# One token tower on one core: the counting products of the expert router are issued behind the probability transposes, and their results are read behind the first normalisation

## The reference

```python
h = _L0_tok_ref(x, W, b, class_token, pos_embed)           # patches @ W.T + b, class token, + pos_embed
h = h + _L0_attn_ref(_layernorm(h), w_qkv, w_proj, b_proj)  # 12 heads of 16, keys within 6 tokens
h = h + _L0_ffn_ref(_layernorm(h), router_w, w1, b1, w2, b2)

# _L0_ffn_ref
probs = softmax(flat @ router_w.T)
top_w, top_i = top_k(probs, 2);  top_w = top_w / top_w.sum(-1)
for e in range(8):
    w_e = sum(top_w * (top_i == e))
    out = out + w_e * (gelu(flat @ w1[e] + b1[e]) @ w2[e] + b2[e])
```

## Time and profile before

| | |
|---|---|
| median of 3 runs | 1693.18 us (1689.94 to 1693.35) |
| the profiled execution | 1697.55 us, of which its span is 1695.8 us |
| TensorE busy | 1491.4 us, 88% of the span |
| weight loads | 1238.1 us, 73% |
| VectorE busy | 1121.2 us, 66% |
| GpSimd busy | 861.2 us, 51% |
| ScalarE busy | 718.4 us, 42% |

### The profile page before, as it was taken

How to read it: one execution, slowest core, us unless ns; L and a number is a source line. 1 busy time by engine, 2 the same in 40 slices (tenths; PEclk the granted TensorE clock), 3 DMA queues, 4 the chain that set the end, 5 groups by cost and what they waited for, 6 DMA issues and landing times. The chain is left out here.

```text
span 1695.8 us, 52298 instructions
## 1 busy us (share of the span) xinstructions
PE 1491.4 (88%) x18345; PEld 1238.1 (73%) x18346; DVE 1121.2 (66%) x2875; ACT 718.4 (42%) x1201; POOL 861.2 (51%) x900
## 2 busy tenths in 40 slices
PE   4777999999999999899562799999999999999995
PEld 4666888888888788788451577777777777777774
DVE  3466777778777776777645466666666666666663
ACT  2443444444444444444421444444444444444441
POOL 3122656656555555555535155545554555455544
PEclk9887999999999999999865799999999999999998
DMA  6654555555555555555422334443444334433432
GB/s 206 205 172 126 157 148 154 153 151 155 144 150 154 150 152 145 143 139 150 113 76 95 93 59 60 60 65 57 59 60 65 57 59 60 65 58 59 59 45 29
DMA packets 190164, 182.64 MB, mean 108 GB/s; under 512 B 86361, under 2 KB 166437, under 8 KB 188989
## 3 DMA queue, kind: packets, MB, share of 16 engines
q1 hardware_dynamic: 125834, 111.46, 23.7%
q0 software_dynamic: 41680, 41.84, 16.8%
q10 hardware_dynamic: 22499, 27.28, 4.9%
HBM read 104.93 MB, written 65.29 MB: 100 GB/s over the span
## 5 line engine op out<-in xcount | busy, mean ns | idle before, releaser
L988 POOL DMA_INDIRECT out<-y,token x219 | 368.5, 1683 | 73.7 <-issue 72.9
L1096 PE MATMUL down<-w_hi,g_hi 128*128 x1314 | 323.7, 246 | 1.9 <-DVE y L1062 1.1
L1098 PE MATMUL down<-w_hi,g_lo 128*128 x1314 | 323.0, 246 | 0.0
L1097 PE MATMUL down<-w_lo,g_hi 128*128 x1314 | 322.9, 246 | 0.0
L1084 PE MATMUL up<-e_xT,w_hi 128*128 128x384 f16 x1314 | 286.7, 327 | 0.0
L1009 ACT ACTIVATE act_out<-up,bias 128x384 f32<-128x384 f32 x438 | 250.9, 581 | 73.3 <-PE up L1084 73.2
L391 POOL DMA_INDIRECT sorted_scratch<-payload,place x212 | 219.5, 1035 | 59.9 <-issue 56.9
L775 PE MATMUL near<-we,patches 128*120 128x192 f32 x1272 | 226.2, 335 | 17.4 <-DMA patches<-in_xt 10.0
L1001 ACT COPY e_xT<-turned 128x1152 f16<-128x1152 f16 x73 | 81.6, 1118 | 353.8 <-PE turned L1076 353.8
L775 PEld LDWEIGHTS near<-we,patches 128*120 128x120 f32 x1272 | 210.2, 187 | 27.8 <-issue 27.7
L1045 DVE TENSOR_TENSOR g_lo<-act_out,g_hi 128x768 f16<-128x768 f32 x219 | 209.9, 958 | 7.6
(11 more groups left out here) (154 smaller groups left out, 2745.9 us busy)
## 6 DMA issues: line engine op xcount, KB each, us to landing
patches<-in_xt SPq DMA_DIRECT2D x53, 720.0 KB
rows<-sorted_scratch SPq DMA_DIRECT2D x73, 301.5 KB, 2.8
v_diag<-v_scratch SPq DMA_DIRECT2D x159, 89.2 KB
v_scratch<-v_rows SPq DMA_DIRECT2D x53, 191.2 KB, 3.0
tab<-tab_scratch SPq DMA_DIRECT2D x53, 180.0 KB
out<-h ACTq DMA_DIRECT2D x52, 180.0 KB
stage<-in_w ACTq DMA_DIRECT2D x8, 1152.0 KB
k_diag<-qk SPq DMA_DIRECT2D x424, 15.8 KB
```

The lines of the kernel that those rows point to most:

```text
L988: pool.indirect_dma_start(out=out, out_offset=bass.IndirectOffsetOnAxis(ap=token[k][:, n:n + 1], axis=0), in_=y[k % 2][:, n, :], in_offset ...
L1096: pe.matmul(dst, g_hi[k % 2][:, m, cols], high, start=(m == 0), stop=False)
L1097: pe.matmul(dst, g_hi[k % 2][:, m, cols], low, start=False, stop=False)
L1098: ins = pe.matmul(dst, g_lo[k % 2][:, m, cols], high, start=False, stop=(m == MF - 1))
```

## The change

On TensorE the block under `if counted:` moves from behind the embedding to behind the turning of the probabilities: behind three groups of transposes. On VectorE the two operations of route part 2 move from ahead of the first normalisation to behind it. Nothing is added or dropped; the semaphores and their values are the same. At t = 8 to 52 all three groups of transposes exist. At t = 54 and 56 there is no turning of xs, at t = 58 and 60 none of the three, and VectorE's first normalisation exists only up to t = 52, so that part 2 moves only there.

```diff
@@ vector, body(t)
                     statistics(h1[f % H_RING], st1, mv1, "1", f + 1)
-                if due:
-                    route_steps(grp, 2)
                 if runs(t, 0):
                     normalise(h1[f % H_RING], mv1, rs1, xn1, "1", f + 1)
...
                 if due:
+                    route_steps(grp, 2)
                     route_steps(grp, 3)
@@ tensor, body(t): the three blocks of transposes now stand ahead of the counting
+                if runs(t, 1):
+                    ...
+                    turn(xs1, token_bank[:].bitcast(F16), ...).then_inc(s["turned1"], 1)
+                if runs(t, 5):
+                    ...
+                    turn(os_, far[:].bitcast(F16), ...).then_inc(s["o_turned"], 1)
+                if runs(t, 4):
+                    pe.wait_ge(s["exp_set"], c + 1)
+                    ...
+                        ins.then_inc(s["prob_turned"], 1)
                 if counted:
                     pe.wait_ge(s["marks_set"], grp + 1)
...
                     ins.then_inc(s["counted"], 1)
-                if runs(t, 1):
-                    ...
-                if runs(t, 5):
-                    ...
-                if runs(t, 4):
-                    ...
                 if runs(t, 6):
```

More of the change, by code:

```diff
@@ L785, in body @@
                 grp, counted = groups(t, 8)
[L786 to L796, removed]
                 if runs(t, 1):
@@ L814, in body @@
                         ins.then_inc(s["prob_turned"], 1)
+                if counted:
+                    pe.wait_ge(s["marks_set"], grp + 1)
+                    pe.wait_ge(s["norm_done"], min(c, BLOCKS))
+                    tiles = 2 * min(2, BLOCKS - 2 * grp)
+                    for n in range(5):
+                        for i in range(min(n + 1, tiles)):
+                            rows = tile_rows(2 * grp + i // 2, i % 2)
+                            ins = pe.matmul(counts[:, n, :], (above16 if i == n else ones16)[0:rows, 0:ROWS], marks[0:rows, i, :],
+                                            start=(i == 0), stop=(i == min(n, tiles - 1)))
+                    ins.then_inc(s["counted"], 1)
                 if runs(t, 6):
```

## The result

The changed kernel takes 1668.64 us (median of 4 runs, 1665.43 to 1672.40), the kernel before 1691.56 beside it (4 runs, 1689.84 to 1693.35). The ratio is 0.9865 [0.9840, 0.9890], 22.9 us less. The profiled execution is the fastest of its four (1665.43, span 1663.6), that of before was above all its other runs (1697.55, span 1695.8), so the two spans differ by 32.2 and the medians by less.

A forecast was written before the change was run, and what follows sets the result against it. TensorE's work and its own waits were taken to bound the kernel, the largest wait being for the marks. Terms 9 + 14.9 + 7.4 - 2 = 29.3 us off 1693.18 gave 1664 us, range 1650 to 1682.

The forecast's parts named there:

- Plain counted bodies: Sixteen ordinary counted bodies: payload's turning starts 0.1 to 0.9 us earlier in each; 9 us, bounds 2.4 and 16.3.
- the first of my two limits: Payload's turning in plain counted bodies can't start before Exp's end plus transposes and products; 0.66 us earlier in one body.
- The six with late marks: Six counted bodies fall to 14.35 us each as transposes fill the wait; 14.9 us, 6.2 of it the clock.
- First counted body and drain: Payload's turning earlier by 2.9 us in the first counted body, 2.3 and 2.2 at t = 54 and 56; together 7.4.
- VectorE's additions: Two additions moved behind the normalisation delay part 3 and L670 by 0.36 us; cost 2 us, bounds 0 and 7.9.
- VectorE becomes the bound: Rival: L676's cover fails, so VectorE's additions cost 7.9 us; 23 off, 1670 us; chance 0.10.
- The wait only moves: Rival: ScalarE's copy or GpSimd's subtraction releases payload's turning at the old time; 17.5 us off, 1676; chance 0.09.
- my signs: Checks named beforehand, such as counted bodies of about 14.4 us and under 0.5 us idle ahead of the counting products.
- The cover by L676: VectorE's L676 ends with GpSimd's L413, hiding L670's delay in counted bodies; cost 0 with it, 7.9 us without.
- The sum: Whole kernel: 9 + 14.9 + 7.4 - 2 = 29.3 us off, giving 1664 us from the median.
- the 1.23 of idle time: TensorE's idle piece in uncounted bodies at clock 1.00, cited against the rival that the clock does not profit.
- the 0.60 ahead of L670: VectorE's idle time in us before L670 in a counted body, cover lost once ScalarE's qk copy comes 0.6 earlier.

The follow-up runs named there:

- second profile of the changed kernel: The changed kernel run once more with no edit, beside the experiments: 1669.91 us (12 runs), 1.0031 of the kernel before.
- second profile of before: The kernel before, profiled once more with no edit, in the conditions of the experiments: 1667.1 us.

## Why the prediction came out as it did

**Plain counted bodies, 9 forecast.** The earlier turning came as drawn, and more of it than forecast. The 9 was itself loose: Exp's end in each of the sixteen gives 0.1 to 1.3 and 11.9 in all by the first of my two limits, under 7 with both. Without the six late ones, 15 bodies in the stretch have a mean of (326.6 - 101.0) / 15 = 15.04, and 14.09 after: 14.3. In the body shown payload's turning came 1.15 us earlier, not 0.58, since Exp itself started 3.58 after the body's start, not 4.12, and ScalarE's copy (L481) was not late there.

**The six with late marks, 14.9.** 101.0 - 6 x 14.09 = 16.4, and no fall of the clock. Marks were still late in five bodies (0.95), as forecast. Inside those bodies the transposes covered them (14.09 against 14.08), but VectorE's queue is late behind them: with the uncounted body that follows, the pair takes 28.74 against 28.36, and in the second profile of the changed kernel 29.24 against 27.96, in seven pairs.

**First counted body and drain, 7.4.** From the end of the last body that embeds to the first expert's product it is 3.2 (127.56 to 124.40), where 4.5 stood. The first counted body brought 0, where 2.9 stood: the turning was 2.83 earlier, and the step that failed is that I let all that followed run at its old speed, while its clock stayed at the lower level longer: 13.6 us in one piece (from 148.4) against 10.2 (from 151.2).

**VectorE's additions, -2, bounds 0 and -7.9.** The uncounted bodies took 5.2 more, which had no term of its own in my sum. I had looked whether L676's end hides the delay, that is, at one body. What counts is the next body, where the softmax stands behind L669 in VectorE's queue and TensorE behind the softmax. No run splits these 5.2 between the two halves of the change. In the later runs both have a part: TensorE's order put 1.04 us on each uncounted body, the additions 0.42 more (13.17, 14.21, 14.63). So the additions are not the whole of it. The step that failed is that I added up what TensorE's counted bodies save as if VectorE could follow.

My rival "VectorE becomes the bound" had the engine right, and its place and price wrong; I had argued against it with VectorE's idle time in uncounted bodies, and that lies behind the softmax, where it doesn't help. "The wait only moves" named payload's turning; the wait moved to Exp, in the uncounted bodies, where none of my signs looked. The cover by L676 is absent in the second profile of the changed kernel: L413 meets an operation ahead of L669 in 16 counted bodies and L675 in none. Without ScalarE's late start the additions' term is 15.7 by the medians, outside my bounds, and the gain of TensorE's order that it is set against is 11, not 31.

**The sum.** 14.3 + 16.4 + 3.2 - 5.2 = 28.7 us in the places of the change, against 29.3. That these agree is in part luck: two terms were low by 5.3 and 1.5, two high by 4.2 and 3.2. The other 3.5 of the 32.2 lie where nothing was changed (2.8 ahead of the first counted body, where the profiles simply differ, the rest behind). And 32.2 is the slowest execution of before against the fastest of the changed kernel; the medians moved by 22.9, 6 less than forecast.

**What it missed.** 1664 was near for kernels run as in the profile I read. There the 1.23 of idle time in the earlier trace rows was mostly, and the 0.60 ahead of L670 in the earlier trace rows wholly, the work of ScalarE's late starts, and I took both for a part of the kernel: in the second profile of before no such idle time stands ahead of L670 but in the five bodies with a fall of the clock. The prediction's gain depends on it: 1.3% with it, 0.3% of loss without.

## What to carry to other kernels

Before a wait is moved out of one engine's queue, follow the engine that feeds the next stage for two rounds of the loop, not one: an unbroken stretch there takes back what the first engine gains. Look in that engine's queue for waits that its other work could fill; moving six operations into such a wait gave 38 us by the medians, 31 by the profiles. An operation five times its median length that begins with another engine's is worth an ordering of its own; here that wait gave 19 us, and TensorE's new order nothing on top. A gain that rests on a delay at a third engine should be measured on another occasion too.

## What was not expected of the hardware

ScalarE started on TensorE's signal about 0.6 us later in the two profiles of one occasion than in the twelve of three others, 0.64 and 0.57 on average against 0.04, with the same program. What causes it, the chip among other things, is open. With it went a difference of 26 us in one kernel's time (1691.6 and 1665.6) and of 1 in the other's (1668.64 and 1669.91); a pause of 0.66 us put there on purpose accounts for 17 of the 26.
